# Attention scores in sets of three heads over three PSUM banks, and three groups of the second feed-forward's features made during attention

## The chip, the cores and the metric

The kernel runs on one core of a Trainium2 chip. The metric is the device time of one execution in microseconds (us); the median of three runs of the kernel before is 288.85 us (288.41 to 289.15). The engines are named as in the profile: PE (matmul), PEld (its weight load), ACT, DVE, POOL and SP.

## What is computed

The block has three residual layers over x (2 batches of 1024 tokens, 128 features): a feed-forward, causal attention with 8 heads of 8, and the same feed-forward again.

```
x = x + 0.5 * ffn(layernorm(x))
x = x + attn(layernorm(x))
x = x + 0.5 * ffn(layernorm(x))

ffn:  h = gelu(x @ w1[e] + b1[e])            for 8 experts e, 128 -> 256
      y = sum over e of (h @ w2[e] + b2[e])  times a gate per token
attn: q, k, v = layernorm(x) * ln_w + ln_b, times w_qkv; q, k to unit length per head
      softmax(8 q k^T, causal) v, times w_out
```

## The kernel before

The 2048 tokens are four groups of 512 (g = 0 to 3). The program is three stages on all engines: the first feed-forward (layer 0, F = g), attention, and the second feed-forward (layer 1, F = 4 + g).

**Feed-forward.** A group has 16 chunks of 128 hidden features. PE does six fp32r matmuls of 512 columns per chunk: three `up` (L471, L474, L477: high and low parts of weights and features) into one of the banks 0 to 3, and three `down` (L489, L492, L494) into bank 4. ACT makes gelu from the bank (L790, L793), DVE the low part of the hidden values (L958). Beside the chunks, group g prepares the features of group g+1: DVE takes the statistics and normalises (`stats`, `aggregate`, `normalise`), POOL makes 1/sqrt(var), PE transposes the four tiles (`ln_transpose`, L442), ACT copies them to `xf` and rounded to `xT_hi` (`ffn_features`), and the low part `xT_lo` is made on POOL (`low_features`, L350). `ffn_groups` writes layer 0 out, and runs layer 1's groups 1 and 2 in a loop (Fori).

**Attention.** The work is four *pairs* (batch, half of the queries), each with two *quads* of four heads. A pair's keys come in *items*: in the first half of a batch three (512 columns, 384 + 128 columns, 256 columns; all on the causal diagonal), in the second half four full ones of 512 columns before those three. One quad and one item is a *quad step*; there are 40. A quad step is two *steps* of two heads, each with a *set* of two PSUM banks out of three such sets (banks 0 to 5).

- PE, `scores(s)` (L602): the score matmuls of two heads, on rows 32j of the array for head j, so that up to four heads lie on different rows. It waits until ACT has emptied that set (exp of step s-3).
- ACT, `exp_scores(s)` (L803): one exp over both banks, 1024 columns (512 in the 256-column item), into one of eight slots of `probs`. It waits for the scores, and for the PV step that read the slot's last content (quad step k-4 for k).
- POOL (L1312): zeroes what the mask hides in the diagonal items.
- PE, `pv(k)` (L625): probabilities times values of a quad step, accumulated in bank 7 or 6 by pair. It stands behind the scores of quad step k+3 in PE's order.

Between PV steps stand 14 *jobs* (a fifteenth, the last projection, comes in the second feed-forward): `fill(n)` on PE writes the bank that the pair doesn't use, `empty(n)` on DVE reads it. They bring the last two groups' q, k and v ("ln", "qkv", "q_stack", "k_stack"), the output projection of finished pairs ("project", L656; before it DVE's `output` normalises the sums and writes `o_feat`), and the features of the second feed-forward's group 0 ("ffn_ln"). After `pv` of quad step 38 come the first three `up` chunks of the second feed-forward, then the last PV step, then layer 1's groups.

PE's, ACT's and DVE's instructions run in the order in which these loops write them, and each engine waits in that order.

Of the kernel before, what the change touches and what calls it, by code (L numbers as in the profile page):

```python
# [56 lines left out]
S_SETS = 3  # L57
P_SLOTS = 8
PV_LAG = 3
# [39 lines left out]
def build(nc, x, ln_w, ln_b, w_qkv, w_out, gate_w, gate_b, rms_w, w1, b1, w2, b2, out):  # L99
# [9 lines left out]
    with ctx:  # L109
# [61 lines left out]
        probs = sb("probs", [P, P_SLOTS, 2, GROUP])  # L171
# [47 lines left out]
        steps = []  # L219
        for u, (b, qg, quad) in enumerate(units):  # L220
            items = score_items(qg)
            for k, item in enumerate(items):
                for pair in range(2):
                    steps.append(dict(unit=u, b=b, qg=qg, quad=quad, pair=pair, item=item, first=(k == 0),
                                      last=(k == len(items) - 1), local=k,
                                      diagonal=any(kt >= GROUP_TILES * qg for kt, *_ in item)))
        masks_until, n_masks = [], 0
        for st in steps:
            n_masks += len(st["item"]) if st["diagonal"] else 0
            masks_until.append(n_masks)  # L230
        quad_steps = len(steps) // 2
        quads_until_unit = [max(i for i, st in enumerate(steps) if st["unit"] == u) // 2 + 1 for u in range(len(units))]
        last_quad = [n - 1 for n in quads_until_unit]
# [5 lines left out]
        pairs = len(units) // QUADS  # L239
        first_of_pair = [0] + [quads_until_unit[QUADS * i - 1] for i in range(1, pairs)]  # L240
# [9 lines left out]

        def score_set(s):

            return s % 2 if s < 4 else (s - 2) % S_SETS

        def set_reader(s):

            return s - 2 if s in (2, 3) else None if s == 4 or s < 2 else s - S_SETS

# [3 lines left out]
        def job_bank(n):  # L262

            at = jobs[n][0]
            return 13 - output_bank(steps[2 * min(at, quad_steps - 1)]["unit"] // QUADS)

        def pair_of_job(n):
            return steps[2 * min(jobs[n][0], quad_steps - 1)]["unit"] // QUADS
# [28 lines left out]

# [50 lines left out]
        def low_features(eng, g):  # L348
            part = ds(g * GROUP, GROUP)
            eng.tensor_tensor(xT_lo[:, part], xf[:, FFN, :], xT_hi[:, part].bitcast(f32), ALU.subtract).then_inc(xT_ready, 1)  # L350
# [79 lines left out]
        def _(pe):  # L430
# [16 lines left out]
            def gate_product(F):  # L447
                pe.wait_ge(xf_done[FFN], F + 1)
                pe.wait_ge(gate_logits_done, F)
                for i in range(GROUP_TILES):  # L450
                    m = pe.matmul(ps[:, BANK_GATE, EXPERTS * i:EXPERTS * i + EXPERTS], xf[:, FFN, P * i:P * i + P],  # L451
# [3 lines left out]
            def up(layer, F, c, g):  # L455
# [8 lines left out]
                if c == 0:  # L464
                    if layer == 1 and isinstance(g, int) and g == 0:
                        pe.wait_ge(xT_ready, F + 1)
                    else:
                        pe.wait_ge(hi_done, F + 1 - layer)
# [39 lines left out]
            def ffn_group(layer, g):  # L508
# [5 lines left out]
                for c in range(CHUNKS):  # L514
# [28 lines left out]
                    if c == at["ln_transpose"] and not last:  # L543
# [10 lines left out]
                    if operands and last and c >= at["att_qkv"]:  # L554
# [37 lines left out]
            def scores(s):  # L592
                st = steps[s]
                if set_reader(s) is not None:
                    pe.wait_ge(exp_done, set_reader(s) + 1)
                for kt, q0, width, at in st["item"]:
# [741 lines left out]
```

## Time and profile before

| | before |
|---|---|
| median of 3 runs | 288.85 us (288.41 to 289.15) |
| profiled execution | 288.67 us, span 286.9 us |
| busy: PE | 274.2 us (96%) |
| busy: ACT | 222.8 us (78%) |
| busy: DVE | 216.9 us (76%) |
| busy: POOL | 87.6 us (31%) |
| granted TensorE clock | 0.999 |

The span runs from the first to the last instruction of the profiled execution; the profiled execution's time is 1.8 us more. Matmuls are pipelined and their ends are modelled, so PE's busy share says little by itself: what PE needs is read from the distance between the starts of its instructions. An idle time in brackets at the end of a row names what ended it.

### The profile page before, as it was taken

What the parts mean: (1) busy time and instruction counts of PE and PEld (TensorE: products, weight loads), DVE (VectorE), ACT (ScalarE), POOL (GpSimd) and SP (SyncE); (2) the same over time, 40 slices, a digit from 0 to 9 for tenths busy, and PEclk for the clock granted to TensorE, in tenths of its full rate; (3) what the DMA queues carried; (4) which work ended last, traced back from release to release, by engine and by line L of the source; (5) the groups of instructions that cost most, each with busy time, mean ns of one, the idle gap of its engine ahead of it and who ended that gap; (6) DMA issues with size and microseconds to landing.
All of it is one profiled execution on the core that took longest, in us unless ns stands there. A gap on an engine that the chain in (4) does not pass through costs nothing.

```text
span 286.9 us, 5191 instructions
## 1 busy us (share of the span) xinstructions
PE 274.2 (96%) x1651; PEld 191.6 (67%) x1651; DVE 216.9 (76%) x573; ACT 222.8 (78%) x346; POOL 87.6 (31%) x155
## 2 busy tenths in 40 slices
PE   8998999999989998899998999999999999999994
PEld 8675788788778886432433432378888888888882
DVE  7699989888989889855588153078788898797765
ACT  2766876868787785999999999976785877677672
POOL 6326203301890383361438321401300310310010
PEclk9999999999999999999999999999999999999999
DMA  5720000000000000000000000000001000100101
GB/s 156 233 73 1 0 1 2 0 0 1 2 1 0 3 1 0 0 2 2 0 3 0 3 0 2 0 2 0 0 2 39 0 0 0 37 0 2 38 0 37
DMA packets 8107, 4.64 MB, mean 16 GB/s; under 512 B 690, under 2 KB 8084, under 8 KB 8084
## 3 DMA queue, kind: packets, MB, share of 16 engines
q1 hardware_dynamic: 8084, 4.35, 5.3%
q8 instruction: 12, 0.20, 0.3%
q14 instruction: 11, 0.09, 0.1%
HBM read 3.30 MB, written 1.05 MB: 15 GB/s over the span
## 4 chain that ended last, share of the span: by engine, by line
PE 73%; POOL 8%; ACT 8%; issue 5%; DVE 4%; DVEq 0%; POOLq 0%; ACTq 0%
PE ps L494 9%; PE ps L489 9%; PE ps L471 8%; PE ps L477 8%; PE ps L474 8%; PE ps L492 8%; PE ps L625 8%; ACT probs L803 5%; PE ps L602 3%; PE ps L664 2%; PE ps L656 2%; PE ps L451 2%; PE ps L580 2%; PE ps L442 2%; POOL rstd L1231 1%
## 5 line engine op out<-in xcount | busy, mean ns | idle before, releaser
L790 ACT ACTIVATE h<-ps,cols 128x512 f32<-128x512 f32 x128 | 87.9, 691 | 48.8 <-PE ps L477 43.5
L958 DVE TENSOR_TENSOR h_lo<-h,h_hi 128x512 fp32r<-128x512 f32 x128 | 92.0, 724 | 29.6 <-ACT h_hi L793 27.1
L803 ACT ACTIVATE probs<-ps 128x1024 f32<-128x1024 f32 (+1 forms) x80 | 67.0, 1013 | 0.6 <-PE ps L602 0.4
L489 PE MATMUL ps<-h_hi,w_hi 128*128 128x512 f32 x128 | 52.9, 413 | 0.3 <-DVE h_hi L956 0.3
L494 PE MATMUL ps<-h_lo,w_hi 128*128 128x512 f32 x128 | 50.9, 398 | 1.4 <-DVE h_lo L958 1.4
L471 PE MATMUL ps<-xT_hi,w_hi 128*128 128x512 f32 (+1 forms) x128 | 50.7, 396 | 0.1
L477 PE MATMUL ps<-xT_lo,w_hi 128*128 128x512 f32 (+1 forms) x128 | 50.0, 391 | 0.0
L492 PE MATMUL ps<-h_hi,w_lo 128*128 128x512 f32 x128 | 50.0, 391 | 0.0
L474 PE MATMUL ps<-xT_hi,w_lo 128*128 128x512 f32 (+1 forms) x128 | 49.9, 389 | 0.0
L793 ACT ACTIVATE h_hi<-ps,cols 128x512 fp32r<-128x512 f32 x72 | 49.2, 683 | 0.0
L1312 POOL TENSOR_SCALAR_AFFINE_SELECT probs<-probs 128x256 f32<-128x256 f32 x64 | 26.0, 431 | 46.5 <-ACT probs L803 46.0
L625 PE MATMUL ps<-probs,v_ones 128*32 128x512 f32 (+3 forms) x384 | 38.8, 495 | 0.0
L494 PEld LDWEIGHTS ps<-h_lo,w_hi 128*128 128x128 f32 x128 | 24.0, 188 | 9.5 <-DVE h_lo L958 4.4
L956 DVE CAST h_hi<-h 128x512 fp32r<-128x512 f32 x56 | 24.9, 444 | 7.0 <-ACT h L790 6.2
L489 PEld LDWEIGHTS ps<-h_hi,w_hi 128*128 128x128 f32 x128 | 24.1, 188 | 5.8 <-DVE h_hi L956 1.6
L471 PEld LDWEIGHTS ps<-xT_hi,w_hi 128*128 128x128 f32 x128 | 24.0, 188 | 5.6 <-ACT h L790 0.4
L477 PEld LDWEIGHTS ps<-xT_lo,w_hi 128*128 128x128 f32 x128 | 24.0, 188 | 5.5 <-DVE xT_lo L1182 0.2
L474 PEld LDWEIGHTS ps<-xT_hi,w_lo 128*128 128x128 f32 x128 | 24.0, 188 | 5.1
L492 PEld LDWEIGHTS ps<-h_hi,w_lo 128*128 128x128 f32 x128 | 24.1, 189 | 3.9
L602 PE MATMUL ps<-qT,kT 32*128 32x512 f16 (+3 forms) x192 | 21.3, 329 | 2.9 <-ACT probs L803 2.3
L602 PEld LDWEIGHTS ps<-qT,kT 32*128 32x128 f16 x192 | 6.5, 91 | 25.2 <-ACT probs L803 15.1
L1231 POOL TENSOR_TENSOR gate_rms<-gate_ms,neg_half 128x4 f32<-128x4 f32 x8 | 10.6, 1320 | 28.5 <-DVE gate_ms L923 28.5
(130 smaller groups left out, 288.4 us busy)
## 6 DMA issues: line engine op xcount, KB each, us to landing
w_raw<-in_L_ffn_w SPq DMA_DIRECT2D x8, 256.0 KB, 4.9
x_sb<-in_L_attn_x SPq DMA_DIRECT2D x3, 256.0 KB, 6.8
out_x<-x_sb SPq DMA_DIRECT2D x3, 256.0 KB, 2.3
x_sb<-in_L_attn_x SPq DMA_DIRECT2D x2, 128.0 KB, 2.2
out_x<-x_sb SPq DMA_DIRECT2D x2, 128.0 KB, 1.8
wout_sb<-in_L_attn_w_out SPq DMA_DIRECT2D x8, 4.0 KB
wqkv_sb<-in_L_attn_w_qkv SPq DMA_DIRECT2D x1, 96.0 KB, 6.0
small<-in_L_ffn_b SPq DMA_DIRECT2D x1, 8.0 KB
```

What stands on the lines that cost most here:

```text
L471: pe.matmul(bank, w1_hi[:, w], xT_hi[:, cols_g], start=True, stop=False)
L474: pe.matmul(bank, w1_lo[:, w], xT_hi[:, cols_g], start=False, stop=False)
L477: pe.matmul(bank, w1_hi[:, w], xT_lo[:, cols_g], start=False, stop=True).then_inc(up_done, 1)
L489: pe.matmul(y, w2_hi[:, w], h_hi[:, c % RING, :], start=(c == 0), stop=False)
L492: pe.matmul(y, w2_lo[:, w], h_hi[:, c % RING, :], start=False, stop=False)
L494: pe.matmul(y, w2_hi[:, w], h_lo[:, c % RING, :], start=False, stop=(c == CHUNKS - 1)).then_inc(down_done, 1)
L602: m = pe.matmul(ps[:, 2 * score_set(s) + hd, at:at + width], kT[rows, st["quad"], k0:k0 + P], qT[rows, st["quad"], qc:qc + width], start=T ...
L625: m = pe.matmul(ps[ROW * j:ROW * j + ROW, bank, q0:q0 + width], v_ones[:, SEQ // P * st["b"] + kt, 4 * st["quad"] + j, :], probs[:, (s + j ...
L790: first = nc.scalar.activation(h[:, slot, :], ps[:, BANK_H + slot, :], ACT.Gelu, bias=bias)
L793: nc.scalar.activation(h_hi[:, slot, :], ps[:, BANK_H + slot, :], ACT.Gelu, bias=bias).then_inc(gelu_done, 1)
L803: nc.scalar.activation(probs[:, s % P_SLOTS, :, 0:width], ps[:, bank:bank + 2, 0:width], ACT.Exp, scale=SCALE).then_inc(exp_done, 1)
L958: dve.tensor_tensor(h_lo[:, slot, :], h[:, slot, :], h_hi[:, slot, :].bitcast(f32), ALU.subtract).then_inc(split_done, 1)
```

## The change

**Sets of three.** The (quad, head) scores of a pair are now laid out as *slots* of one PSUM bank each, 144 in all; the 256-column items of both quads share four slots (two heads of 256 columns in one bank). Slots are cut into 50 sets: three of two slots (the first two sets' scores and the third's are made at the end of layer 0), 45 of three, one of two, one of one. Sets alternate between banks 0 to 2 and 3 to 5, so that two sets are in PSUM where there were three. ACT makes one exp per set. `probs` holds five sets of three slots (15) where it held eight of two (16).

PE's order is written by turns: turn n makes the scores of set n, then the PV steps that are due in turn n, each followed by its job. A PV step is due three turns after the last set that it reads, four turns if it is masked (`turn_of_step`). The scores of set n wait for the exp that last used its banks (n-2); the exp of set n waits for the scores and for the last PV step that reads set n-5, whose place in `probs` it takes.

**Features in attention.** Two jobs more, "ffn_ln" 1 and 2: the features of groups 1 and 2 of the second feed-forward are normalised, transposed and split during attention, on DVE, POOL (1/sqrt) and PE; the unrounded features of these two go to the memory of the raw weights (`features`). Job "k_stack" 3 moves from quad step q2 + 1 to q1 + 13, "ffn_ln" 0 from q3 + 5 to q2 + 1. In layer 1 only group 2 prepares features (`turns`).

**Loops written out.** `ffn_groups` has no Fori any more.

```diff
-S_SETS = 3
-P_SLOTS = 8
-PV_LAG = 3
+SET = 3
+P_SETS = 5
+EARLY_SETS = 3
+PV_LAG, PV_LAG_MASKED = 3, 4
...
-        probs = sb("probs", [P, P_SLOTS, 2, GROUP])
+        probs = sb("probs", [P, P_SETS, SET, GROUP])
...
+        sizes = [2] * EARLY_SETS
+        sizes += [SET] * ((len(slots) - sum(sizes)) // SET - 1) + [2, 1]
...
+            return 2 * (n % 2) if n < EARLY_SETS else SET * (n % 2)
...
+        last_set = [set_of_slot[st["slot"] + 3] for st in steps]
+        turn_of_step = [last_set[k] + (PV_LAG_MASKED if st["diagonal"] else PV_LAG) for k, st in enumerate(steps)]
+        turn_of_step = [max(turn_of_step[:k + 1]) for k in range(quad_steps)]
...
-                (q1 + 12, "q_stack", LAST), (q2 + 1, "k_stack", LAST),
-                (q2 + 4, "project", (1, 0)), (q2 + 5, "project", (1, 1)),
-                (q3 + 1, "project", (2, 0)), (q3 + 2, "project", (2, 1)), (q3 + 5, "ffn_ln", 0),
+                (q1 + 12, "q_stack", LAST), (q1 + 13, "k_stack", LAST), (q2 + 1, "ffn_ln", 0),
+                (q2 + 3, "project", (1, 0)), (q2 + 4, "project", (1, 1)),
+                (q3 + 1, "project", (2, 0)), (q3 + 2, "project", (2, 1)), (q3 + 5, "ffn_ln", 1),
+                (q3 + 8, "ffn_ln", 2),
...
-            group(0)
-            if layer == 0:
-                for g in range(1, GROUPS - 1):
-                    group(g)
-            else:
-                with eng.Fori(1, GROUPS - 1) as g:
-                    group(g)
-            group(GROUPS - 1)
+            for g in range(GROUPS):
+                group(g)
+        def turns(layer, g):
+            return g < LAST if layer == 0 else g == LAST - 1
...
+            y_transposes(LAST, BANK_YT_LAST)
+            next_job, next_step = 0, 0
+            for n in range(EARLY_SETS, max(turn_of_step) + 1):
...
+                    scores(n)
+                while next_step < quad_steps and turn_of_step[next_step] == n:
+                    if next_step == quad_steps - QUADS:
+                        pe.wait_ge(exp_done, len(sizes) - 1)
                         for c in range(LAG):
                             up(1, GROUPS, c, 0)
+                    pv(next_step)
+                    if jobs[next_job][0] == next_step:
                         fill(next_job)
                         next_job += 1
+                    next_step += 1
...
+            def exp_scores(n):
+                act.wait_ge(scores_done, n + 1)
+                if n >= P_SETS:
+                    act.wait_ge(pv_done, max(steps_reading(n - P_SETS)) + 1)
+                bank = set_bank(n)
+                nc.scalar.activation(probs[:, n % P_SETS, 0:sizes[n], :], ps[:, bank:bank + sizes[n], :], ACT.Exp,
                                      scale=SCALE).then_inc(exp_done, 1)
...
+                if (kind, arg) == ("k_stack", LAST):
+                    normalise(FFN, GROUPS, 0)
+                if (kind, arg) == ("project", (1, 1)):
+                    dve.wait_ge(job_emptied, n + 1)
+                    first_stats(GROUPS + 1)
+                if (kind, arg) == ("project", (2, 1)):
+                    normalise(FFN, GROUPS + 1, 1)
+                    dve.wait_ge(job_emptied, n + 1)
+                    first_stats(GROUPS + 2)
...
+                if (kind, arg) == ("ffn_ln", 1):
+                    normalise(FFN, GROUPS + 2, 2)
```

How PE's order changes, inside the second pair. L602 is a score matmul, L625 a PV matmul, L580 a job; "x3" counts equal rows. Before, the scores of quad step 16, then PV step 13 and its job "q_stack" 2:

```order
L602 MATMUL ps<-qT,kT 128x512 [waits exp_done]
L602 MATMUL ps<-qT,kT 128x512
L602 MATMUL ps<-qT,kT 128x512 [waits exp_done]
L602 MATMUL ps<-qT,kT 128x512
L625 MATMUL ps<-probs,v_ones 32x512 [waits exp_done]
L625 MATMUL ps<-probs,v_ones 32x512 x3
L580 MATMUL ps<-ident,q_stack 128x128 [waits stack_done,job_emptied]
L580 MATMUL ps<-ident,q_stack 128x128 x7
```

Four heads' scores, in two sets that each wait for an exp, stand ahead of a PV step and its job. With the change, turns 23 and 24 (L659 a score matmul, L682 a PV matmul, L632 the job "k_stack" 2):

```order
L659 MATMUL ps<-qT,kT 128x384 [waits exp_done]
L659 MATMUL ps<-qT,kT 128x384
L659 MATMUL ps<-qT,kT 128x256
L659 MATMUL ps<-qT,kT 128x128 x2
L659 MATMUL ps<-qT,kT 128x256
L682 MATMUL ps<-probs,v_ones 32x512 [waits mask_done]
L682 MATMUL ps<-probs,v_ones 32x512 x3
L632 MATMUL ps<-ident,k_stack 128x128 [waits stack_done,job_emptied]
L632 MATMUL ps<-ident,k_stack 128x128 x7
L659 MATMUL ps<-qT,kT 128x256 [waits exp_done]
L659 MATMUL ps<-qT,kT 128x256 x5
L682 MATMUL ps<-probs,v_ones 32x512 [waits mask_done]
```

Scores wait once per set of three heads, and the PV step that frees the place in `probs` for set n stands behind the scores of set n and, in the next turn, behind the job.

ACT's exps before, in the third pair's run of full items, and with the change, from set 5 to the end:

```order
L803 ACTIVATE probs<-ps 128x1024 [waits pv_done,scores_done] x12
L803 ACTIVATE probs<-ps 128x2x256 [waits pv_done,scores_done] x2
```

```order
L855 ACTIVATE probs<-ps 128x1536 [waits pv_done,scores_done] x43
L855 ACTIVATE probs<-ps 128x1024 [waits pv_done,scores_done]
L855 ACTIVATE probs<-ps 128x512 [waits pv_done,scores_done]
```

80 exps become 50, over the same 73,728 columns.

The job "ffn_ln" 2 and the end of the attention on PE, with the change (turns 47 to 49; L704 transposes normalised tiles):

```order
L682 MATMUL ps<-probs,v_ones 32x512 [waits mask_done]
L682 MATMUL ps<-probs,v_ones 32x512 x3
L704 MATMUL ps<-ident,xn 128x128 [waits xn_done_ffn,job_emptied]
L704 MATMUL ps<-ident,xn 128x128 x3
L659 MATMUL ps<-qT,kT 128x256 [waits exp_done]
L659 MATMUL ps<-qT,kT 128x256 x3
L682 MATMUL ps<-probs,v_ones 32x512 [waits mask_done]
L682 MATMUL ps<-probs,v_ones 32x512 x3
L659 MATMUL ps<-qT,kT 128x256 [waits exp_done]
L659 MATMUL ps<-qT,kT 128x256
```

In layer 1 the four transposes of `ln_transpose` now stand in group 2 alone; before, they stood in group 0 and in the loop's body.

## Rows read from the trace of the kernel before

**Rows 1.** Sums of stretches: us, then busy us (instructions) of each engine, PEclk, DMA.

```profile
131.60:184.90 53.30, 51.35 (x514) 18.07 (x516) 27.04 (x69) 52.70 (x64) 20.36 (x49) 1.00 0.01 2
188.75:282.50 93.75, 93.75 (x443) 76.80 (x439) 77.17 (x195) 67.87 (x110) 13.11 (x13) 1.00 0.03 9
```

**Rows 2.** Timeline of ACT in attention: start, us, engine, line, count, idle before.

```profile
119.15 1.02 ACT L803 ACTIVATE probs<-ps 128x1024 f32<-128x1024 f32 x1
...
126.48 1.13 ACT L803 ACTIVATE probs<-ps 128x1024 f32<-128x1024 f32 x1
...
126.48 9.38 ACT L803 ACTIVATE probs<-ps 128x1024 f32<-128x1024 f32 x10
...
154.96 0.60 ACT L803 ACTIVATE probs<-ps 128x512 f32<-128x512 f32 x1 [0.37 <-PE ps L602]
...
183.60 0.73 ACT L803 ACTIVATE probs<-ps 128x512 f32<-128x512 f32 x1
...
184.08 0.74 ACT L803 ACTIVATE probs<-ps 128x512 f32<-128x512 f32 x1
```

**Rows 3.** Timeline of PE in the second pair; a row's price is the distance to the next start.

```profile
131.65 1.06 PE L625 MATMUL ps<-probs,v_ones 128*32 128x512 f32 x8
132.65 0.66 PE L647 MATMUL ps<-ident,xn 128*128 128x128 f32 x4
133.24 0.40 PE L602 MATMUL ps<-qT,kT 32*128 32x512 f16 x4
...
134.56 0.71 PE L656 MATMUL ps<-wout_sb,o_feat 128*128 128x128 f32 x4
...
141.22 0.92 PE L650 MATMUL ps<-wqkv_sb,xf 128*128 128x192 f32 x4
142.07 0.40 PE L602 MATMUL ps<-qT,kT 32*128 32x512 f16 x4
142.40 0.64 PE L625 MATMUL ps<-probs,v_ones 128*32 128x256 f32 x8
...
145.14 0.62 PE L580 MATMUL ps<-ident,q_stack 128*128 128x128 f16 x8
...
154.63 0.29 PE L602 MATMUL ps<-qT,kT 32*128 32x256 f16 x4
```

**Rows 4.** Timeline of DVE: four tiles' statistics; first and last instruction of `output`, second pair.

```profile
139.59 0.86 DVE L889 BATCH_NORM_STATS2 bn_part<-x_sb 128x6 f32<-128x128 f32 x4
140.48 0.38 DVE L898 BATCH_NORM_AGGREGATE mean_var<-bn_part 128x2 f32<-128x6 f32 x4
...
155.56 0.72 DVE L1121 STREAM_TRANSPOSE o_blocks<-ps 128x512 f32<-128x512 f32 x1
...
157.15 0.71 DVE L1135 STREAM_TRANSPOSE o_feat<-o_scaled 128x512 f32<-128x512 f32 x1
```

**Rows 5.** Timeline of PE where attention ends and the second feed-forward begins.

```profile
185.91 0.50 PE L471 MATMUL ps<-xT_hi,w_hi 128*128 128x512 f32 x1
...
188.18 0.64 PE L625 MATMUL ps<-probs,v_ones 128*32 128x256 f32 x8
188.75 0.50 PE L471 MATMUL ps<-xT_hi,w_hi 128*128 128x512 f32 x1
```

**Rows 6.** Timeline of PE in the second feed-forward, around both transposes and the loop's entry.

```profile
204.31 0.39 PE L477 MATMUL ps<-xT_lo,w_hi 128*128 128x512 f32 x1
...
205.21 0.40 PE L492 MATMUL ps<-h_hi,w_lo 128*128 128x512 f32 x1
...
212.97 0.39 PE L477 MATMUL ps<-xT_lo,w_hi 128*128 128x512 f32 x1
213.19 0.39 PE L471 MATMUL ps<-xT_hi,w_hi 128*128 x1
...
228.01 0.39 PE L477 MATMUL ps<-xT_lo,w_hi 128*128 x1
...
229.01 0.40 PE L492 MATMUL ps<-h_hi,w_lo 128*128 128x512 f32 x1
```

More of the change, by code:

```diff
@@ new lines, in banks_free_after, with steps_reading, mask_regions @@
+        def banks_free_after(n):
+            mine = range(set_bank(n), set_bank(n) + sizes[n])
+            users = [m for m in range(n) if any(bank in mine for bank in range(set_bank(m), set_bank(m) + sizes[m]))]
+            return max(users) + 1 if users else 0
+        def steps_reading(n):
+            return [k for k, st in enumerate(steps) if any(set_of_slot[st["slot"] + j] == n for j in range(4))]
+        def mask_regions(n):
+            regions = []
+            for i, slot in enumerate(slots_of[n]):
+                if not slots[slot]["diagonal"]:
+                    continue
+                starts = sorted(at + base for _, base in slots[slot]["heads"] for *_, at in slots[slot]["item"])
+                if regions and regions[-1][2] == starts and regions[-1][1] == i:
+                    regions[-1][1] = i + 1
+                else:
+                    regions.append([i, i + 1, starts])
+            return regions
@@ L234, in build @@
+        turn_of_step = [last_set[k] + (PV_LAG_MASKED if st["diagonal"] else PV_LAG) for k, st in enumerate(steps)]
+        turn_of_step = [max(turn_of_step[:k + 1]) for k in range(quad_steps)]
+        steps_until_pair = [sum(st["pair"] <= pair for st in steps) for pair in range(pairs)]
+        last_mask_of_pair = [max(n for n in range(len(sizes)) if any(slots[i]["pair"] == pair and slots[i]["diagonal"] for i in slots_of[n]))
+                             for pair in range(pairs)]
         halves = ((0, 1), (2, 3))
@@ L542, in ffn_group @@
                         scores(0)
-                    if c == at["ln_transpose"] and not last:
+                    if c == at["ln_transpose"] and turns(layer, g):
                         if layer or not first:
@@ L846, in ffn_group @@
                         affine_features(g - 1)
-                    if c == at["ln_copy"] and not last:
+                    if c == at["ln_copy"] and turns(layer, g):
                         ffn_features(layer, F + 1, g + 1)
@@ L874, in _ @@
             ffn_groups(nc.scalar, 0, lambda g: ffn_group(0, g))
-            for s in range(2, len(steps)):
-                exp_scores(s)
+            for n in range(2, len(sizes)):
+                exp_scores(n)
             for c in range(LAG):
@@ L1035, in ffn_group @@
                 for c in range(CHUNKS):
-                    if c == at["ln_aggregate"] and not last:
+                    if c == at["ln_aggregate"] and turns(layer, g):
                         wait_stats(FFN, F + 1)
@@ L1043, in ffn_group @@
                         weight_parts(2 + c // 5)
-                    if not last:
+                    if turns(layer, g):
                         if c == at["ln_stats"][0]:
@@ L1054, in ffn_group @@
                             if c == at["ln_normalise"][half]:
[L1055 removed]
+                                normalise(FFN, F + 1, g + 1, halves[half])
                     for half in range(2):
@@ L1263, in ffn_group @@
                     inverse_lengths(pool, g - 2, range(2))
-                if not last:
+                if turns(layer, g):
                     ln_once(F + 1)
@@ L1274, in ffn_group @@
                     low_parts(pool, g - 2)
-                if not last:
-                    pool.wait_ge(hi_done, F + 2 - layer)
-                    low_features(pool, g + 1)
+                if turns(layer, g):
+                    pool.wait_ge(hi_done, F + 2 - LAST * layer)
+                    low_features(pool, F + 1, g + 1)
             pool.memset(ones[:, :], 1.0).then_inc(const_self, 1)
```

206 lines of the change are left out of this document (104 added, 102 removed).

## The prediction

> **What bounds the kernel now.** I read the sums by stretch first. In attention ACT is busy 52.70 of 53.30 us and PE 51.35, in the second feed-forward PE 93.75 of 93.75 at full granted clock [rows 1]. So attention is a chain of exps with PE close behind, and after it only PE counts. The timeline of ACT gives the price of an exp [rows 2]. Ten queued exps of 1024 columns take 9.38 us and the first alone 1.13, so one more costs (9.38 - 1.13) / 9 = 0.917. The last two, of 512 columns, end at 183.60 + 0.73 = 184.33 and 184.08 + 0.74 = 184.82: 0.49 each. So 512 columns more cost 0.425, and what doesn't depend on the columns is 0.065. An exp that finds ACT empty takes 1.02 (1024) or 0.60 (512) from its start, 0.10 more than a queued one. PE's prices are distances between starts [rows 3]: scores 0.33 (142.07 to 142.40), a PV step 1.00 (its result after 1.065), one of 256 columns 0.57 (0.64), a job "ln" or "ffn_ln" 0.59, "project" 0.64, "qkv" 0.85, a stack 0.55 (a row's length less the 0.07 by which it overlaps the next). A handoff between engines costs about 0.04: scores that end at 154.63 + 0.29 let an exp start at 154.96 [rows 2, 3].
>
> Before, the exps from 119.15 on would end at 119.15 + 0.10 + 62 x 0.917 + 16 x 0.49 = 183.9 without a stall; they end at 184.82 [rows 2], so stalls cost 0.9 us with three sets in PSUM. The second feed-forward's own stream starts 3.93 us later, at 188.75 [rows 5].
>
> **Fewer exps.** The columns stay, 30 exps go. An exp of three banks should cost 0.917 + 0.425 = 1.34 queued, 1.44 on an empty ACT. From exp 2 on there are 45 of these, two of 1024 and one of 512: 60.4 + 1.83 + 0.49 = 62.7 against 64.7. Gain 30 x 0.065 = **2.0 us**, and without any stall ACT would end at 119.15 + 0.10 + 62.7 = 182.0. The Trainium skill ("ScalarE: Activation LUTs", Rules for kernel authors) budgets about 0.3 us per ACTIVATE and 0.83 ns per element. Its slope agrees with the 0.425 us per 512 columns; by its fixed part the gain would be 30 x 0.3 = 9 us, and queued exps in this trace don't show it.
>
> **The new wait.** `probs` has five places, and a masked PV step comes four turns after its last set. Counted over the 50 sets, in 17 turns (5, 7, 8, 10, 11, 23, 24, 26, 27, 28, 30, 31, 32, 34, 35, 47, 48) the exp of set n needs the PV step of the same turn n; I call them ring turns. That PV step stands on PE behind the scores of set n, and these wait for exp n-2, whose banks they take. Before, the needed PV step stood a whole quad step earlier in PE's order. Write E for an exp's end:
>
> - Ring turn with PE in time: exp n starts at E(n-2) + 0.04 + 0.33 + 1.065 + 0.04 = E(n-2) + 1.475 and ends 1.44 later, at 2.915; two queued exps need 2.684. Loss 0.23. This holds for turns 5, 7, 10, 23, 26, 30, 34, 47: **1.85 us**. A ring turn right behind another (8, 27, 31) loses nothing more, since PE's turn of 0.33 + 1.00 is as long as an exp.
> - Ring turn behind a ring turn with a job J: PE arrives J later, and nothing takes it up: loss J. Turns 24 (0.55), 32 and 48 (0.59 each): 1.7. Turn 35 comes behind "project" (0.64) and holds half PV, "project", half PV in place of one PV: 0.64 + (0.57 + 0.64 + 0.64 - 1.065) = 1.4. Turn 28 holds half PV, "q_stack" 3, half PV: 0.7, and 0.25 since PE had to wait for exp 26: 0.9. Turn 11, two halves: 0.14. Sum **4.2 us**.
>
> **PE late without the ring.** With two sets in PSUM, PE may be late by one exp less its handoffs. Turns 18 and 19 hold scores, PV and "qkv": 2 x 2.18 = 4.36, and the scores of set 20 are read 0.43 later, at 4.79 after those of set 18 began; three exps from E(16) end at 4.03, less 0.04 and the 0.10 of overlap 3.9: loss 0.9. By the same reckoning turn 12 loses 0.6 (turn 11 ends with a full PV step and "ln"), turn 15 0.25 (two projections), turns 38 and 39 1.05. The last is two projections again, and in addition DVE: `output` (155.56 to 157.86, 2.30 us) now stands behind the statistics of group 1 (1.24) [rows 4], so that "project" (2,0) waits for `o_feat` on PE. Sum **2.8 us**. Set 3 needs banks 3 to 5 and its scores stand behind the transposes of layer 0's last result; before, exp 3 had its scores by then: 0.2.
>
> Stalls together 1.85 + 4.2 + 2.8 + 0.2 = 9.0, so ACT ends at 182.0 + 9.0 = **191.0** in place of 184.82. The table load and the gelus behind it are covered as now.
>
> **The end of attention.** After PV step 35 ACT needs 1.02 + 0.49 for the last two exps. PE needs scores 0.33, two PV steps 2.0, three `up` chunks 2.27 (185.91 to 188.18) and two half PV steps 1.14 [rows 3, 5]: 5.74, that is 4.2 behind ACT in place of 3.93. The second feed-forward's stream starts at 195.2, **6.45 us later**.
>
> **The second feed-forward.** It loses two times four transposes: from the third `up` matmul to the second `down` matmul 0.90 and 1.00 us against two normal distances of 0.455 [rows 6]: 0.44 + 0.55 = **1.0 us** gained. What ACT, DVE and POOL lose there was hidden behind PE. The two jobs that replace it are in the turns above (42 and 47); the former fits, the latter is the 0.59 of turn 48. The loop written out brings nothing: its first matmul starts 0.22 after the one before, the normal distance [rows 6]. The Trainium skill ("Runtime: NRT & Kernel Launch", Instruction fetch mechanics) says that a taken branch whose target has not been fetched stalls the engine; no such stall is in these rows, so I take none back. A move on POOL and DVE costs nothing elsewhere: in attention they are busy 20.36 and 27.04 of 53.30 us [rows 1].
>
> **Sum.** +6.45 - 1.0 = +5.45 on the profiled execution's 288.67: **294.1 us**. The median of the runs, 288.85, is 0.18 higher, inside their spread; I leave it.
>
> **Bounds of what no row shows.** An exp over three banks: between 1.34 (slope) and 1.44 (if each starts on an empty ACT); the stalls shrink little when it grows, so the upper end adds up to 2 us. Scores of three heads: 0.33 lies between four heads in one go (0.33) and slower mixes of shapes; 0.1 more per turn would add 2 to 3 us, since PE's turns become longer than an exp. If they ran wholly under other matmuls, up to 0.13 less per turn, the start at 195.2 would move by about 2.2.
>
> **Rivals.**
>
> - *PE hides its jobs as it does today* (the ring costs what I say, the other lateness nothing). For it: before, the same jobs cost only 0.9 of stalls. Against: there were three sets then. 294.1 - 2.8 = 291.3.
> - *The engines run decoupled* (the other sign): a PV result comes early enough for every exp, and only ACT's own 62.7 us count. Place: the ring turns; it needs the PV result by E(n-1) - 0.10, 0.23 earlier than above, and jobs that fit in the slack of turns without a PV step (one in four). Then ACT ends at 182.2, the stream starts 3.93 later, 2.65 earlier than now: 288.67 - 2.65 - 1.0 = 285.0. From stalls of 3.6 us in all (9.0 - 5.45) the change breaks even. Against it stands that the scores ahead of that PV step can't start before E(n-2).
> - *Scores cost more*: sets that mix 512, 384 + 128 and 2 x 256 columns take 0.43 in place of 0.33. About 297.
> - *The fixed part of an exp is larger than queued rows say*: at most 1.02 - 0.85 = 0.17 for an exp that starts on an empty ACT [rows 2], so 30 exps bring 5.1 in place of 2.0: 291.0. The Trainium skill ("ScalarE: Activation LUTs", Rules for kernel authors) would lie on this side.
> - *The gains cancel the stalls*, by a mixture of these: 288.7.
>
> **Chances.** Forecast (292.3 to 296) 0.56, jobs hidden 0.16, scores dearer 0.10, larger fixed part 0.03, cancelling 0.04, decoupled 0.11. The range reaches over the first four, 290.0 to 297.0, and leaves out somewhat under 2 in 10. A difference of 0.3% is about what a measurement of this kernel can tell from none: faster 0.12, same 0.03, slower 0.85.
>
> **What would show it.** Exps of 1536 columns with starts 1.33 apart where queued. ACT idle in some 25 places in attention, most often ended by a PV matmul (ring turns) or a score matmul, the largest near turns 35, 28 and 20; PE idle in attention ended by exps, before scores; the table load near 191.0; the second feed-forward's first stream near 195.2, its length 1.0 less, without new gaps. I am wrong if ACT's idle time in attention stays below 4 us, or if the exps of three banks are far from 1.34.

## The result, and the profile after

The changed kernel takes 297.55 us (median of four runs, 295.4 to 299.91) against 288.77 us before on the same chip. Without the slowest run, at 299.91 us, it takes 1.028 times the time (95% interval 1.0242 to 1.0318). It is slower, as forecast. The profiled execution took 295.4 us against the 294.1 of the prediction; the median lies 0.55 us above the range's upper end. The two come apart together with TensorE's granted clock, which differs from run to run: 1.000 in the two runs at 295.4 and 295.52, 0.974 and 0.977 in the two at 299.59 and 299.91. No term of the sum was for that.

Sums of stretches of the changed kernel, in the columns of [rows 1]: the start of attention, the rest of it, and the second feed-forward to the end of the span.

```profile
119.19:131.60 12.41, 8.08 (x99) 2.94 (x103) 6.85 (x28) 11.28 (x10) 6.46 (x16) 1.00 0.00 1
131.60:192.20 60.60, 53.07 (x534) 18.33 (x527) 36.02 (x100) 53.76 (x40) 21.84 (x46) 1.00 0.01 1
196.50:293.70 97.20, 93.54 (x435) 76.30 (x435) 73.12 (x175) 66.24 (x108) 8.10 (x7) 1.00 0.04 12
```

ACT, busy in 52.70 of 53.30 us before [rows 1], is now busy in 53.76 of 60.60: the work is much the same, the gaps are new. Their sum stands in the list of costliest groups, who ended them in the list of waits between 119 and 196 us (total, times, longest).

```profile
L855 ACT ACTIVATE probs<-ps 128x1536 f32<-128x1536 f32 (+2 forms) x50 | 67.0, 1403 | 8.0 <-PE ps L682 5.6 <-PE ps L659 2.4
```

```profile
PE ps L659 <- ACT probs L855: 10.4, 14, 1.4
...
ACT probs L855 <- PE ps L682: 5.6, 13, 1.3
...
ACT probs L855 <- PE ps L659: 2.4, 6, 0.7
```

ACT and PE wait for each other in turn: exps for PV steps (L682) 13 times and for scores (L659) six times, scores for exps 14 times. The timeline of ACT (the columns of [rows 2]) shows where; a row holds as many exps as ran without a gap.

```profile
120.55 2.79 ACT L855 ACTIVATE probs<-ps 128x1536 f32<-128x1536 f32 x2 [0.35 <-PE ps L659]
123.57 2.79 ACT L855 ACTIVATE probs<-ps 128x1536 f32<-128x1536 f32 x2 [0.23 <-PE ps L682]
126.68 4.13 ACT L855 ACTIVATE probs<-ps 128x1536 f32<-128x1536 f32 x3 [0.32 <-PE ps L682]
...
146.06 4.13 ACT L855 ACTIVATE probs<-ps 128x1536 f32<-128x1536 f32 x3 [0.72 <-PE ps L659]
...
159.13 2.79 ACT L855 ACTIVATE probs<-ps 128x1536 f32<-128x1536 f32 x2 [0.93 <-PE ps L682]
...
168.52 1.45 ACT L855 ACTIVATE probs<-ps 128x1536 f32<-128x1536 f32 x1 [0.23 <-PE ps L682]
171.27 4.13 ACT L855 ACTIVATE probs<-ps 128x1536 f32<-128x1536 f32 x3 [1.30 <-PE ps L682]
...
177.71 10.85 ACT L855 ACTIVATE probs<-ps 128x1536 f32<-128x1536 f32 x8 [0.51 <-PE ps L659]
188.79 1.45 ACT L855 ACTIVATE probs<-ps 128x1536 f32<-128x1536 f32 x1 [0.23 <-PE ps L682]
190.69 1.51 ACT L855 ACTIVATE probs<-ps 128x1024 f32<-128x1024 f32 x2 [0.46 <-PE ps L682]
```

Eight exps in 10.85 us and one in 1.45 make (10.85 - 1.45) / 7 = 1.34 for a queued exp of three banks. From here on the time that an exp loses is the distance from the end of the exp before to its own end, less this price; it is the gap and, after a gap, another 0.11, since an exp that finds ACT empty takes 1.45. The last exp ends at 190.69 + 1.51 = 192.20 (184.82 before, [rows 2]), and the second feed-forward's own stream starts at 196.38 (188.75 before, [rows 5]), as the timeline of PE shows:

```profile
119.54 0.63 PE L557 MATMUL ps<-ident,yT 128*128 128x128 f32 x4 [0.98 <-ACT yT L865]
...
122.06 0.39 PE L659 MATMUL ps<-qT,kT 32*128 32x384 f16 x6 [1.34 <-ACT probs L855]
122.38 1.07 PE L682 MATMUL ps<-probs,v_ones 128*32 128x512 f32 x8
...
196.38 0.50 PE L523 MATMUL ps<-xT_hi,w_hi 128*128 128x512 f32 x1
```

So the stream starts 7.63 us later. From there to the end of the span it takes 293.7 - 196.38 = 97.32 us, before 286.9 - 188.75 = 98.15: 0.83 less. Together that is the 6.8 us by which the span grew.

### The profile page after: what moved, and what is told of

The parts are those of the page before. It is cut to its first block, busy times and chain, and to the rows that moved or that the text cites. A ratio compares the mean times of both kernels' runs of the same rounds, so it can differ in the third digit from the quotient of the medians.

```text
span 293.7 us, 4898 instructions
## 1 busy us (share of the span) xinstructions
PE 272.2 (93%) x1651; PEld 189.7 (65%) x1651; DVE 220.4 (75%) x579; ACT 220.8 (75%) x312; POOL 85.0 (29%) x148
## 4 chain that ended last, share of the span: by engine, by line
PE 70%; POOL 10%; ACT 10%; DVE 5%; issue 4%; DVEq 0%; ACTq 0%; POOLq 0%
PE ps L546 9%; PE ps L541 9%; PE ps L523 8%; PE ps L529 8%; PE ps L526 8%; PE ps L544 8%; ACT probs L855 8%; PE ps L682 8%; PE ps L659 3%; POOL rstd L1292 2%; PE ps L713 2%; PE ps L503 2%; PE ps L494 1%; PE ps L622 1%; DVE h_lo L1010 1%
## 5 line engine op out<-in xcount | busy, mean ns | idle before, releaser
L855 ACT ACTIVATE probs<-ps 128x1536 f32<-128x1536 f32 (+2 forms) x50 | 67.0, 1403 | 8.0 <-PE ps L682 5.6
L523 PE MATMUL ps<-xT_hi,w_hi 128*128 128x512 f32 x128 | 50.6, 396 | 0.0
L529 PE MATMUL ps<-xT_lo,w_hi 128*128 128x512 f32 x128 | 49.9, 390 | 0.0
L526 PE MATMUL ps<-xT_hi,w_lo 128*128 128x512 f32 x128 | 49.9, 390 | 0.0
L682 PE MATMUL ps<-probs,v_ones 128*32 128x512 f32 (+3 forms) x384 | 38.6, 495 | 0.2 <-POOL probs L1373 0.2
L1373 POOL TENSOR_SCALAR_AFFINE_SELECT probs<-probs 128x384 f32<-128x384 f32 (+2 forms) x59 | 25.5, 457 | 39.8 <-ACT probs L855 39.8
L1008 DVE CAST h_hi<-h 128x512 fp32r<-128x512 f32 x56 | 24.3, 435 | 8.4 <-ACT h L843 7.1
L659 PE MATMUL ps<-qT,kT 32*128 32x512 f16 (+3 forms) x192 | 19.1, 328 | 10.4 <-ACT probs L855 10.4
L659 PEld LDWEIGHTS ps<-qT,kT 32*128 32x128 f16 x192 | 5.4, 91 | 28.6 <-ACT probs L855 17.3
```

What stands on the lines that cost most here:

```text
L523: pe.matmul(bank, w1_hi[:, w], xT_hi[:, cols_g], start=True, stop=False)
L526: pe.matmul(bank, w1_lo[:, w], xT_hi[:, cols_g], start=False, stop=False)
L529: pe.matmul(bank, w1_hi[:, w], xT_lo[:, cols_g], start=False, stop=True).then_inc(up_done, 1)
L659: m = pe.matmul(ps[:, bank, base + at:base + at + width], kT[rows, quad, k0:k0 + P], qT[rows, quad, qc:qc + width], start=True, stop=True)
L682: m = pe.matmul(ps[ROW * j:ROW * j + ROW, bank, q0:q0 + width], v_ones[:, SEQ // P * st["b"] + kt, 4 * st["quad"] + j, :], held[:, st["bas ...
L855: nc.scalar.activation(probs[:, n % P_SETS, 0:sizes[n], :], ps[:, bank:bank + sizes[n], :], ACT.Exp, scale=SCALE).then_inc(exp_done, 1)
```

## The experiments

All kernels were compared with the kernel before on the same chip.

**again: the spread.** The changed kernel as it is.

> The changed kernel once more, to see whether its runs differ by granted clock. In four runs two took 295.4 and 295.5 us at a granted clock of 1.00 and two 299.6 and 299.9 us at 0.97. Theory: PE waits up to 1.4 us several times in attention, and in some runs the clock is granted at its lower level for a stretch there or right behind it; then again about half of the runs are near 295.5 and half near 299.7, and a profile of a run of the second kind shows the lower level in or behind attention. Rival: it was the chip of that job; then all runs are near 295.5.

298.73 us (295.52, 297.62, 299.85, 301.37; ratio 1.037, 1.0309 to 1.0433). Time and granted clock again go together: 1.000 at 295.52, 0.988 at 297.62, 0.977 at 299.85, 0.971 at 301.37. Its profile is of the run at 295.52, at full clock throughout.

**lag3 and six: the ring.** Two ways to take the ring away. In lag3 masked PV steps come a turn earlier, in six `probs` gets a sixth place.

```diff
-PV_LAG, PV_LAG_MASKED = 3, 4
+PV_LAG, PV_LAG_MASKED = 3, 3
```

```diff
-P_SETS = 5
+P_SETS = 6
```

> The changed kernel with masked PV steps due three turns after their last set, not four: no exp then needs a PV result of its own turn. Theory (the ring wait): of the 10.2 us by which exps lose time in the changed kernel, the isolated ring turns (about 8 x 0.33) and the job lengths behind ring turns (about 4) go, PE's other lateness (2.8) stays and some of the lost time comes back as waits for masks: 290 to 292 us, and the gaps before exps that a PV matmul ended are gone. Rival 1 (two sets in PSUM alone are to blame, the ring only passes it on): 294 or more, the gaps are now ended by score matmuls. Rival 2 (masks now hold PE up as much): 295.

> The changed kernel with six places for sets in probs, the lag of four turns kept: the exp needs a PV step one turn back at the latest. Theory: the gaps before exps that a PV matmul ended (ring turns) go, PE's lateness behind jobs stays or grows, since PV steps and jobs stand where they stood: about 2 us less, 293 to 294 us. Rival (the ring is the whole loss): as good as the version with lag 3, 291 us or less. Rival 2 (the ring isn't binding): 295.5.

291.65 us (ratio 1.0089, 1.0067 to 1.0111) and 293.96 us (1.018, 1.0149 to 1.021), inside the ranges expected. In six part of the time goes with the clock, which no range had in it: three of its four runs were at 0.986 to 0.988, and the one at 0.998 took 293.23 us. In both profiles no exp waits for a PV step any more. For lag3 (the profile is of its slowest run, 292.35 us), first the waits of ACT and PE in attention, then ACT's timeline, whole:

```profile
ACT probs L855 <- PE ps L659: 5.9, 6, 3.3
...
PE ps L632 <- DVE k_stack L430: 1.9, 1, 1.9
```

```profile
120.57 16.23 ACT L855 ACTIVATE probs<-ps 128x1536 f32<-128x1536 f32 x12 [0.35 <-PE ps L659]
137.18 6.90 ACT L855 ACTIVATE probs<-ps 128x1536 f32<-128x1536 f32 x5 [0.39 <-PE ps L659]
144.80 10.85 ACT L855 ACTIVATE probs<-ps 128x1536 f32<-128x1536 f32 x8 [0.72 <-PE ps L659]
158.92 9.72 ACT L855 ACTIVATE probs<-ps 128x1536 f32<-128x1536 f32 x7 [3.27 <-PE ps L659]
169.28 5.69 ACT L855 ACTIVATE probs<-ps 128x1536 f32<-128x1536 f32 x4 [0.63 <-PE ps L659]
175.48 13.60 ACT L855 ACTIVATE probs<-ps 128x1536 f32<-128x1536 f32 x11 [0.51 <-PE ps L659]
```

The gaps at turns 15 (137.18), 20 (144.80) and 39 (175.48) stay: they are among those that I had put down to PE's jobs and not to the ring. Two more of those, at turns 12 and 38, are gone. At turn 28 (158.92) the gap grew from 0.93 to 3.27. ACT came there earlier, but DVE's stacks did not: PE waited 1.85 us for `k_stack`, and then ran at the lower of its two levels (1.2 GHz), as the sums by stretch show.

```profile
154.00:155.90 1.90, 0.06 (x4) 0.02 (x1) 1.73 (x4) 1.65 (x2) 1.67 (x4) 1.00 0.00 0
155.90:157.00 1.10, 1.09 (x16) 0.60 (x16) 0.45 (x1) 0.00 (x0) 0.72 (x3) 1.00 0.00 0
157.10:160.40 3.30, 3.10 (x28) 1.38 (x28) 2.17 (x7) 1.48 (x2) 0.00 (x0) 0.50 0.00 0
```

In six the clock fell at the start of attention, during the second of two waits of PE of 0.98 and 1.35 us (the second ends at 121.62); the same sums:

```profile
118.00:121.00 3.00, 1.30 (x15) 0.70 (x14) 2.46 (x9) 2.49 (x3) 0.67 (x2) 0.99 0.00 0
121.00:127.70 6.70, 6.08 (x40) 1.18 (x44) 5.10 (x21) 6.23 (x6) 5.52 (x14) 0.50 0.01 2
```

For 6.7 us PE works at half speed, busy for 6.08 of them. The changed kernel has the same two waits (119.54 and 122.06 above), so this place came under suspicion for its spread.

**fill: the clock at the start.** Three times four matmuls more, in waits of PE, whose results nobody reads.

```diff
+            def idle_matmuls(bank):
+                for _ in range(4):
+                    pe.matmul(ps[:, bank, :], kT[:, 0, 0:P], qT[:, 0, 0:GROUP], start=True, stop=True)
...
+            idle_matmuls(7)
             y_transposes(LAST, BANK_YT_LAST)
...
+                if n == 5:
+                    idle_matmuls(7)
+                if n == 7:
...
+                    idle_matmuls(6)
```

> The changed kernel with twelve matmuls more, whose results nobody reads: four into a free bank in each of three places at the start of attention where PE waits for ACT (0.98 us before the last transposes of layer 0, 1.34 us before the scores of set 5, 1.37 us before those of set 7). Four take about 0.9 us, so each fits into its wait. In the eight runs of the changed kernel three are at 295.4 to 295.5 with the granted clock at 1.000, and five at 297.6 to 301.4 with 0.971 to 0.988. Theory A (the clock falls at the start of attention, because PE waits there, and gives the runs above 295.5): now all runs are at 295.2 to 296.0, clock 0.997 or more; median 295.5. Rival (it falls elsewhere, at the waits of turns 24 to 35): the spread stays, median 296.5 to 299.

295.24 us, all five runs between 294.74 and 295.33, clock 0.996 to 1.000 (ratio 1.0212, 1.0198 to 1.0226). With work in these three waits the spread of 6 us is gone; one run, 294.74, lies below the range expected. PE at the start; L743 are the new matmuls:

```profile
118.51 1.04 PE L743 MATMUL ps<-qT,kT 128*128 128x512 f16 x4
...
120.69 1.04 PE L743 MATMUL ps<-qT,kT 128*128 128x512 f16 x4
121.99 0.39 PE L659 MATMUL ps<-qT,kT 32*128 32x384 f16 x6 [0.26 <-ACT probs L866]
...
123.66 1.04 PE L743 MATMUL ps<-qT,kT 128*128 128x512 f16 x4
125.10 0.39 PE L659 MATMUL ps<-qT,kT 32*128 32x256 f16 x5 [0.40 <-ACT probs L866]
```

So the time of the changed kernel has two parts: 295.3 us at full clock, which the instruction order explains, and up to 6 us that came with a lower clock in some runs and did not come back once PE had work in its first waits. Two things stay open. None of the five slower runs has a profile, so where their clock fell is not seen: from their mean clock (0.988 to 0.971 over some 298 us, half of full at the lower level) I estimate 7 to 17 us at the lower level, more than the one stretch of 6.7 us in six. And fill ran on another chip than the run again. The kernel before takes the same time on both (288.97 and 289.01 us), but the changed kernel itself was not run on the chip of fill.

**two: sets of two.** The changed kernel with two heads to a set over three pairs of banks.

```diff
-SET = 3
-P_SETS = 5
-EARLY_SETS = 3
-PV_LAG, PV_LAG_MASKED = 3, 4
+SET = 2
+P_SETS = 8
+EARLY_SETS = 4
+PV_LAG, PV_LAG_MASKED = 6, 6
...
-            return 2 * (n % 2) if n < EARLY_SETS else SET * (n % 2)
+            return 2 * (n % 2) if n < EARLY_SETS else 2 * ((n - 2) % 3)
```

> The changed kernel with sets of two slots over three pairs of banks, eight places in probs and PV steps six sets back, as in the kernel before; the new slots (72 exps, not 80 or 50), the features in attention and the loops written out stay. Theory: the stalls come from sets of three with two in PSUM, and the rest of the change is sound: 1.0 us less in the second feed-forward, 8 x 0.065 = 0.5 less in exps, the two jobs of 0.59 hidden: 287.3 us (286.7 to 288.2), exps in attention losing about 1 us. Rival (the features in attention are what costs, by DVE and the jobs): 291 or more, with the gaps near the projections and the features' jobs.

289.18 us (ratio 1.0012, 1.0 to 1.0024): no difference from before, where I had expected 287.3. The size of the sets and what goes with it (places, lag, number of sets in PSUM) is thus worth 295.4 - 289.2 = 6.2 us, nearly the whole loss. In lag3 one number, the turn of the masked PV steps, was worth 295.4 - 291.65 = 3.75 us, so the sets alone are not the whole of it. Of the missing 1.9 us most was lost in one gap of ACT, 1.45 us before the exp at 157.91. First ACT, then PE's timeline there, then the first stack job at the same place in the kernel before:

```profile
157.91 2.87 ACT L854 ACTIVATE probs<-ps 128x1024 f32<-128x1024 f32 x3 [1.45 <-PE ps L658]
```

```profile
155.53 0.61 PE L631 MATMUL ps<-ident,q_stack 128*128 128x128 f16 x8 [0.81 <-DVE k_stack L429]
156.06 0.64 PE L681 MATMUL ps<-probs,v_ones 128*32 128x256 f32 x8
156.92 0.62 PE L631 MATMUL ps<-ident,k_stack 128*128 128x128 f16 x8 [0.22 <-DVE qT L1194]
157.47 0.40 PE L658 MATMUL ps<-qT,kT 32*128 32x384 f16 x8
158.32 1.07 PE L681 MATMUL ps<-probs,v_ones 128*32 128x512 f32 x8 [0.45 <-DVE kT L1197]
```

```profile
154.09 0.61 PE L580 MATMUL ps<-ident,q_stack 128*128 128x128 f16 x8 [0.81 <-DVE k_stack L378]
```

The exp waits for the scores at 157.47. PE waits 0.81 us for DVE's stacks as it did before, but then the scores came right behind the query stack. Now both stack jobs stand ahead of the scores, and since they share one bank, the second waits 0.22 us for DVE to copy the first out. The next pair's first PV step, which uses the bank, waits for the second (0.45); that is behind the scores, and ACT runs on without a gap.

**loops: the loops alone**, in the kernel before.

```diff
-            group(0)
-            if layer == 0:
...
-            group(GROUPS - 1)
+            for g in range(GROUPS):
+                group(g)
```

> The kernel before, with nothing changed but the group loop of the second feed-forward written out. Theory (the loop's entry shows the normal distance of 0.22 us between matmuls): no difference, 288.7 to 289.2 us, ratio 0.999 to 1.001. Rival (a taken branch stalls PE somewhere in the second feed-forward): 0.3 to 1 us less, 288.0 to 288.6.

289.21 us, ratio 1.001 (0.9998 to 1.0022): nothing gained.

**feat, feat_k and lag3k: the list of jobs.** feat is two with the 80 exps of before (a narrow piece of each quad in a set of its own). Its edit beside two (and the exps cut to the width of their pieces):

```diff
-                together = width < GROUP
+                together = False
```

feat_k on top of feat, and lag3k on top of lag3:

```diff
-                (q1 + 12, "q_stack", LAST), (q1 + 13, "k_stack", LAST), (q2 + 1, "ffn_ln", 0),
-                (q2 + 3, "project", (1, 0)), (q2 + 4, "project", (1, 1)),
+                (q1 + 12, "q_stack", LAST), (q2 + 1, "k_stack", LAST), (q2 + 2, "ffn_ln", 0),
+                (q2 + 4, "project", (1, 0)), (q2 + 5, "project", (1, 1)),
```

> The changed kernel with sets of two heads over three bank pairs, 80 exps of the widths before (64 of 1024, 16 of 512 columns), eight places, PV steps three quad steps behind: what is left of the change is the features made in attention with its list of jobs, the order of the pieces, and the loops. The run two, of the same kind but with 72 exps, came out at 289.18: its second feed-forward is 0.9 us shorter, and its attention lost 2.0 us more than the kernel before, 1.56 of them at one place, where the key stack stands right behind the query stack in the list of jobs. Theory A (the list of jobs is the cause): that loss is here too, 288.9 - 0.9 + 2.0 = 290.0, range 289.4 to 290.4. Theory B (the loss in two comes from its packing of the narrow pieces into full banks): 288.9 - 0.9 = 288.0, range 287.8 to 288.3.

> As feat, but the job of the last key stack back at its place of before (one step into the third pair, four steps behind the query stack), and the jobs ffn_ln 0 and project (1,0), (1,1) one step later each. Theory A (the list of jobs is the cause): the 1.56 us go, 290.0 - 1.5 = 288.5, range 288.0 to 288.8. Theory B: no difference from feat, 288.0.

> As lag3 (sets of three, masked PV steps three turns behind, 291.65 us), with the last key stack back at its place of before and the three jobs behind it one step later. In the profile of lag3 ACT lost 3.4 us at turn 28, where PE stands before the two stacks, 2.1 of them in waits, and then runs 3.4 us at the half clock. Theory (the stacks side by side are the cause): most of this goes, 291.65 - 2.0 to 3.0 = 288.7 to 289.7. Rival (the wait for DVE's stack of before q_stack, 1.85 us, which stays): 291.0 to 291.7.

292.56 us (1.0131, 1.0113 to 1.0149), 294.62 us (1.0208, 1.0174 to 1.0243) and 293.23 us (1.0157, 1.0137 to 1.0178). All three missed: neither theory was right. PE in feat, at the start and before the stacks:

```profile
121.54 0.61 PE L658 MATMUL ps<-qT,kT 32*128 32x384 f16 x4 [0.52 <-ACT probs L855]
122.08 1.94 PE L681 MATMUL ps<-probs,v_ones 128*32 128x512 f32 x8
...
157.34 0.61 PE L631 MATMUL ps<-ident,q_stack 128*128 128x128 f16 x8 [1.92 <-DVE k_stack L429]
```

A PV step of 1.94 in place of 1.06 us is one at the lower clock, and the clock fell here at both places. The 1.92 us come from DVE. Its chain from the last query and key job to the stacks is some 10 us long. PE stands ready for the stacks 9.5 us after the start of that job here (145.90 to 155.42), 10.3 us in the kernel before and 10.8 us in two, and it waits 0.81 us in both of those. My reading is the order of the pieces. In the order of before that job stood beside a narrow PV step (0.57 us). In the new order, in which the narrow pieces of both quads come last, it stands beside whole ones (1.00), and the narrow ones lie between it and the stacks. But two has the new order as well, without the longer wait, so the order alone is not shown to be the cause. In feat_k PE waits 1.92 us at the same place and another 1.07 us for DVE's normalised tiles before "ffn_ln" 0. In lag3k the wait for DVE stays (1.86 us), and the key stack, put further back, now delays the scores that need it by 0.79 us: with sets of three they are read earlier relative to the PV steps.

**feat_q, best, best_fill: the features alone.** feat_q has the order of before in all of attention, and in it the two further jobs "ffn_ln".

```diff
+            for quad in range(QUADS):
+                for k, item in enumerate(items):
...
+                (q1 + 12, "q_stack", LAST), (q2 + 1, "k_stack", LAST), (q2 + 3, "ffn_ln", 0),
+                (q2 + 4, "project", (1, 0)), (q2 + 5, "project", (1, 1)),
```

> The instruction order of the kernel before in all of attention (80 exps, three sets of two banks, one quad finished before the next, stacks and projections at their old places), and in it two jobs more, ffn_ln of the second and third group, as in the changed kernel. So the features alone, with the loops. feat and feat_k, where the pieces stood in the new order, were 3.6 and 5.7 us slower than the kernel before, in part because the query and key job of group 3 stood beside whole PV steps and no longer beside a narrow one, so that DVE's stacks came late for PE, which then waited 1.9 us; and the clock fell in both. Theory A (the features cost nothing by themselves, the order does): the second feed-forward is 0.9 us shorter, 288.9 - 0.9 = 288.0, range 287.8 to 288.3. Theory B (PE has no room for two more jobs of 0.59 us: 51.35 of 53.30 us are busy): 288.9 - 0.9 + 1.2 = 289.2, range 288.8 to 289.4.

294.72 us (1.0194, 1.017 to 1.0218), far from both theories. Here too the runs differ with the clock: 293.17 and 293.36 us at 0.994 and 0.993, the other three 294.72 to 295.21 at 0.981 and 0.982. First POOL's timeline, then PE's:

```profile
174.92 0.20 POOL L1288 TENSOR_TENSOR var_eps<-mean_var,ln_eps 128x4 f32<-128x4 f32 x1 [6.39 <-DVE mean_var L943]
175.20 1.01 POOL L1285 TENSOR_TENSOR rstd<-var_eps,neg_half 128x4 f32<-128x4 f32 x1
176.17 2.92 POOL L1366 TENSOR_SCALAR_AFFINE_SELECT probs<-probs 128x256 f32<-128x256 f32 x8
```

```profile
176.99 1.07 PE L674 MATMUL ps<-probs,v_ones 128*32 128x512 f32 x8 [3.28 <-POOL probs L1366]
```

POOL stands for 6.39 us at the statistics of group 2, with eight masks queued behind it, and PE waits 3.28 us for those. In the order of before the last pair's first masks come right here; in the new order all its masks come at its end. In the changed kernel POOL stands as long for statistics, 6.4 us, and PE waits only 0.2 us for masks. So the order of the pieces is no detail of the sets of three: it makes room for POOL's part of the features. best moves that part behind these masks, and the statistics of group 1 behind the third pair's `output`; best_fill also fills the first two waits of PE, with two and three matmuls.

```diff
-                if (kind, arg) == ("project", (1, 1)):
+                if (kind, arg) == ("project", (2, 0)):
...
-                if n == last_mask_of_pair[2]:
+                if n == last_mask_of_first_quad:
                     ln_once(GROUPS + 1)
                     ln_once(GROUPS + 2)
```

> As feat_q (294.72 us), with two moves. In feat_q POOL stood at L1288 for 6.39 us, waiting for DVE's statistics of group 2 with the masks of the last pair's first quad queued behind; PE waited 3.28 us for these masks and then ran at the half clock. Here POOL's two pieces of work for the features stand behind those masks. And DVE's statistics of group 1 stand behind the output of the third pair and its first projection, where in feat_q PE waited 1.00 us for that output. Theory A (order alone made feat_q slow; the features themselves cost nothing): 288.9 - 0.9 = 288.0, range 287.7 to 288.4, faster than both kernels. Theory B (two more jobs of 0.59 us find no room on PE): 289.2, range 288.7 to 289.6.

> As best (288.78 us), with five matmuls whose results nobody reads, two in PE's wait of 0.66 us before the last transposes of layer 0 and three in its wait of 0.72 us before the scores of set 6; each piece is shorter than its wait. Eleven runs of best had a granted clock of 0.990 to 0.992 in eight cases or so; in its profile PE stood at the half clock from 121.5 to 124.9 us, right behind these waits, and ACT lost 0.87 us at exp 8. Theory A (these waits bring the clock down): the clock stays at 0.996 or more in nearly all runs, and 288.78 - 0.87 = 287.9, range 287.7 to 288.3, faster than both kernels by about 0.3%. Rival (the clock falls here for another reason, or the wait then shows up elsewhere): 288.5 to 289.0.

best: 288.78 us, ratio 1.0001 (0.9991 to 1.0011), inside theory B's range. In its profile, of its slowest run (289.26 us), exps lose the 0.89 us of before at the same places, 0.81 more at three places beside the moved jobs (0.26, 0.18, 0.37), and 0.87 at exp 8, where the clock is low; the second feed-forward gives 0.9 of that back. best_fill: 288.27 us, ratio 0.9983 (0.9974 to 0.9993): the fastest of all, 0.17% below the kernel before, which is inside the expected range, but less than the 0.3% of its middle. Its clock is 0.997 to 1.000 in all twelve runs. At the start, in sums by stretch, first best, then best_fill:

```profile
118.50:121.50 3.00, 1.61 (x16) 0.80 (x12) 2.50 (x10) 3.00 (x5) 1.30 (x4) 1.00 0.00 0
121.50:124.90 3.40, 3.40 (x22) 0.57 (x26) 3.09 (x17) 2.63 (x4) 2.88 (x7) 0.50 0.02 5
```

```profile
118.20:121.20 3.00, 2.95 (x20) 1.13 (x19) 2.67 (x10) 2.93 (x5) 1.28 (x4) 1.00 0.00 0
121.20:124.60 3.40, 3.16 (x40) 1.00 (x38) 3.09 (x16) 3.40 (x6) 3.05 (x9) 1.00 0.02 5
```

PE's busy time ahead goes from 1.61 to 2.95 of 3.00 us, and the clock behind it stays. The gain, 0.5 us, is less than the 0.87 that exp 8 lost in best's profile, and runs of best at 1.000 took 288.67 and 288.77 us; how much of the 0.5 is the clock remains open. The two kernels also ran on different chips, each beside the kernel before.

## Why the prediction held, and where not

- **Fewer exps.** Right: 1.34 us for a queued exp of three banks, to the hundredth. The rival with a larger fixed part falls; an exp on an empty ACT has one of 1.45 - 1536 x 0.00083 = 0.17. The Trainium skill ("ScalarE: Activation LUTs", Rules for kernel authors) budgets about 0.3 us per ACTIVATE besides its elements, for one whose bias is an operand, a condition that I had left out. The trace agrees for a gelu, which has one (0.69 us for 512 columns, 0.265 without the 0.425 of its columns); these exps have none, and show 0.065 queued and 0.17 on an empty ACT.
- **Isolated ring turns: the term that was mis-sized.** The eight lost 0.34 each (7 and 26: 0.43), 2.9 us in place of 1.85. PV step 122.38 ends at 123.45, its exp starts at 123.57: this handoff takes 0.12 us, not 0.04. From exp 3's end (120.55 + 1.45 = 122.00) on: 0.06 to the scores, 0.32 for them, 1.07 for the PV step, 0.12, 1.45 for the exp; 3.02 against two queued exps in 2.68 is the 0.34. I had taken the handoff from scores to exps for one from PV steps too.
- **Ring turns behind jobs.** 4.1 us against 4.2: turns 24, 32, 48, 35, 28 lost 0.53, 0.57, 0.56, 1.40, 1.04; turn 11 lost nothing in place of 0.14. That the ring carries these losses is shown by lag3 and six, where the waits for PV steps are gone. Not all of the 7.0 us of the ring came back: in the profile of lag3 ACT ends at 189.08 in place of 192.20, 3.1 us earlier, since at turn 28 it now waits 3.27 us for scores.
- **PE late without the ring.** 2.7 us against 2.8: turn 12 0.40, 15 0.28, 19 and 20 0.91, 38 and 39 1.07. The start: 0.46 in place of 0.2, since exp 3's scores come 0.35 us after ACT is free.
- **Sum of stalls** 10.2 against 9.0; ACT's end 192.20 against 191.0; the tail 4.18 against 4.2. The 1.2 us are the ring turns (1.0) and the start (0.3); the other terms nearly cancel. ACT was idle before 19 exps, where I had named some 25 places, with the largest gaps at the turns named (35, 28 and 20).
- **Second feed-forward.** 0.83 us gained against 1.0: up to the last transposes (289.80, before 283.10) PE's stream is 0.93 us shorter, and 0.10 is lost behind them. In attention its two jobs were not free: even in best exps lose 0.81 us more beside the moved jobs. That work moved to POOL and DVE costs nothing, I had argued from their busy shares. It held in the changed kernel (0.2 us of waits for masks) and not in feat_q (3.28 us): what counts is what is queued behind the moved work.
- **Loops.** Nothing, as said; no stall of the branch shows.
- **The clock: the part that the sum lacked.** I had said that the clock of PE was full in the profile, and took it for given. [Rows 1] begin at 131.60 and say nothing of the start, and no row could show what more idle time on PE would do. Five of the eight runs of the changed kernel are at a lower clock and 2 to 6 us longer than the other three, and that is what puts the median past the range. The Trainium skill ("TensorE: Matmul & The Clock Gate", A second HAM failure mode: psum-queue depth-cycling) describes a kernel in which PE idles briefly between groups of matmuls and the clock goes to and fro. This case agrees in kind: the only edit of fill is work in such waits, and its five runs lie within 0.6 us.
- **The rivals.** "Decoupled" fell with the rows above: the scores can't start before exp n-2 ends, and 14 waits of PE for exps show it. "Jobs hidden" fell with the 2.7 us of PE's lateness. "Scores dearer" was not seen: 0.32.

## What to carry over

Fewer, longer instructions on the bounding engine did not pay here, because they took away the spare buffer between it and the engine that feeds it: going from three sets of two banks to two sets of three gained 2 us of exps and cost 10 us of waits (0.9 before), which could be counted turn by turn from the profile of before. 3.75 us of the loss hang on the turn of the masked PV steps alone (lag3), so count the places and the lag as well as the sets. When a job moves, look at what it now stands beside, and at what is queued behind each wait on every engine, POOL's masks included. And where a change makes TensorE wait, the granted clock belongs in the sum: in fill, a few matmuls that nobody reads, put into the waits, went with times that repeat.

## What was not expected of the hardware

- The granted clock fell to 1.2 GHz during or behind waits of PE of 0.5 to 2 us: 0.98 and 1.35 us in six, 0.66 and 0.52 in feat, 1.85 in lag3. It doesn't fall each time: the profiles of the changed kernel and of two have the same waits at the start at 1.000, and lag3k has a wait of 1.86 us at lag3's place without a fall. What decides it between equal waits is not shown.
- At 1.2 GHz a PV step's matmuls take 1.94 us in place of 1.06 (feat), so half the clock nearly doubles them, and ACT, which waits for them, loses only what isn't covered: 0.87 us for 3.4 us at the lower level in best.
- An exp after a PV step starts 0.12 us after the step's modelled end (122.38 + 1.07 to 123.57), one after scores 0.04 ([rows 2, 3]).
